# A gated cross-attention block with routed experts: GpSimd's low-weight rows behind VectorE's second norm, routing groups and scatters earlier, tables over four steps

## What is computed

```
x = x + tanh(g_xattn) * xattn(ctx, layernorm(x))
    # s = layernorm(ctx)*g1+b1; t = layernorm(.)*g2+b2; q = t Wq; k = s Wk; v = s Wv
    # softmax(q k^T / sqrt(8)) v, 16 heads, then Wfc
xf = layernorm(x)
gates = sigmoid(xf @ Wg); vals, idx = top_k(gates, 2); vals = vals / vals.sum()
shared = (silu(xf @ Ws1) * (xf @ Ws3)) @ Ws2
routed = sum over the two chosen experts: weight * (silu(xf @ We1) * (xf @ We3)) @ We2
x = x + tanh(g_ffn) * (shared + routed) / 3
```

## Time and profile before

| | us |
|---|---|
| median of 3 runs | 461.3 |
| lowest, highest | 459.54, 461.4 |
| the profiled execution | 458.93 |
| its span | 457.1 |

### The profile page before, as it was taken

How to read it: one execution, slowest core, us unless ns; L and a number is a source line. 1 busy time by engine, 2 the same in 40 slices (tenths; PEclk the granted TensorE clock), 3 DMA queues, 4 the chain that set the end, 5 groups by cost and what they waited for, 6 DMA issues and landing times.

```text
span 457.1 us, 10667 instructions
## 1 busy us (share of the span) xinstructions
PE 359.4 (79%) x3718; PEld 269.3 (59%) x3718; DVE 344.0 (75%) x866; ACT 264.9 (58%) x601; POOL 279.4 (61%) x375
## 2 busy tenths in 40 slices
PE   0689999997998969899869710999999999999400
PEld 0356666665765647676658600777777777778300
DVE  2559999999999998998848820576777777777447
ACT  1257777776687746687656600355555555556244
POOL 3373666666379966888647773017777777777700
PEclk9999999999799988899979865799999999999855
DMA  4920699991001110000001155113236666541179
GB/s 110 275 77 3 261 375 377 391 385 41 13 27 49 36 48 25 27 25 26 25 23 42 49 217 165 52 52 94 93 95 231 232 231 230 210 184 52 47 264 298
DMA packets 39331, 62.36 MB, mean 136 GB/s; under 512 B 5936, under 2 KB 23344, under 8 KB 39280
## 3 DMA queue, kind: packets, MB, share of 16 engines
q1 hardware_dynamic: 32704, 51.12, 32.6%
q0 software_dynamic: 4992, 10.30, 6.7%
q10 hardware_dynamic: 1584, 0.27, 0.4%
HBM read 18.32 MB, written 31.56 MB: 109 GB/s over the span
## 4 chain that ended last, share of the span: by engine, by line
PE 41%; DVE 25%; issue 13%; POOL 13%; ACT 4%; DMA 3%; POOLq 0%; DVEq 0%; SPq 0%; ACTq 0%
POOL expert_rows L545 7%; PE ps L1215 6%; PE ps L1216 5%; PE ps L1217 5%; DVE row_max L935 5%; PE ps L1252 3%; DVE inv_sum L976 3%; PE ps L1158 3%; POOL token_sums L622 3%; PE ps L1112 3%; DVE norm L900 2%; PE ps L1240 2%; PE ps L1238 2%; PE ps L1239 2%; DVE x_sb L1061 2%
## 5 line engine op out<-in xcount | busy, mean ns | idle before, releaser
L622 POOL DMA_INDIRECT token_sums<-prob,y_at x92 | 94.5, 1027 | 60.7 <-DVE prob L1035 38.8
L545 POOL DMA_INDIRECT expert_rows<-c_sb,pos x64 | 64.3, 1005 | 16.9 <-issue 16.8
L587 POOL TENSOR_TENSOR k_mask<-k_st,head_mask 128x512 f32<-128x512 f32 x32 | 33.5, 1046 | 43.8 <-ACT k_st L695 43.6
L739 ACT ACTIVATE h_hi<-prob 128x512 fp32r<-128x512 f32 x62 | 38.3, 634 | 36.5 <-DVE prob L998 36.5
L732 ACT ACTIVATE probT<-ps 128x512 f32<-128x512 f32 x62 | 36.9, 598 | 30.6 <-PE ps L1217 27.0
L1112 PE MATMUL ps<-k_mask,qT 32*64 32x256 f32 x512 | 46.0, 431 | 9.4 <-DVE prob L941 7.7
L998 DVE TENSOR_TENSOR prob<-ps,probT 128x512 f32<-128x512 f32 x62 | 40.2, 684 | 13.9 <-ACT probT L732 10.9
L935 DVE TENSOR_REDUCE row_max<-ps 128x16 f32<-128x1024 f32 x32 | 38.9, 1216 | 11.0 <-PE ps L1112 10.9
L1003 DVE TENSOR_TENSOR h_lo<-prob,h_hi 128x512 fp32r<-128x512 f32 x62 | 40.5, 689 | 3.4 <-ACT h_hi L739 0.4
L1019 DVE TENSOR_TENSOR xT_lo<-ps,xT_hi 128x512 fp32r<-128x512 f32 x23 | 15.9, 692 | 35.9 <-ACT xT_hi L744 35.9
L703 ACT ACTIVATE probT<-ps 128x512 f32<-128x512 f32 x64 | 35.2, 595 | 10.5 <-PE ps L1158 10.4
(11 more groups left out here) (164 smaller groups left out, 977.1 us busy)
## 6 DMA issues: line engine op xcount, KB each, us to landing
expert_rows<-zeros SPq DMA_DIRECT2D x36, 520.0 KB, 5.2
c_sb<-expert_rows SPq DMA_DIRECT2D x23, 260.0 KB, 2.7
wbuf_hi<-w_hi SPq DMA_DIRECT2D x15, 384.0 KB, 2.9
wbuf_lo<-w_lo SPq DMA_DIRECT2D x15, 384.0 KB, 3.4
w_raw<-in_L_ffn_We_dram SPq DMA_DIRECT2D x24, 128.0 KB, 4.2
c_sb<-token_sums SPq DMA_DIRECT2D x8, 256.0 KB, 4.7
xT_lo<-token_sums SPq DMA_DIRECT2D x8, 256.0 KB, 4.9
out_dram<-x_sb SPq DMA_DIRECT2D x8, 256.0 KB, 4.9
```

The lines of the kernel that those rows point to most:

```text
L545: pool.indirect_dma_start(out=xs, out_offset=bass.IndirectOffsetOnAxis(pos[:, k, i:i + 1], 0), in_=c_sb[:, i, :], in_offset=None).then_inc ...
L622: pool.indirect_dma_start(out=ys, out_offset=bass.IndirectOffsetOnAxis(y_at[:, s, k:k + 1], 0), in_=yrows[:, s % 2, k * D:(k + 1) * D], in ...
```

## The change

Four things. GpSimd's step has a new wait, for xn2_ready of tile t-4, ahead of w_lo and the scale piece, in steps 4 to 14, where no tile is scattered. The routing tables are moved up: GATE_STEP by one step, COUNT_STEP and RANK_STEP by two, and all five parts of `routing` run in COUNT_STEP itself. Scatters start at step 15 instead of 18, one tile a step, and so the table for the steps behind NT = 32 is another one; tiles 24 to 27 no longer wait for unit 4. The tables are written in steps 0 to 3 in four parts. TensorE waits for gate_exp behind the logits matmul instead of ahead of it, and has a new wait for pos_ready at step 35.

```
-        GATE_STEP = [14, 22, 30, 34, None]
-        COUNT_STEP = [16, 24, 32, 36, None]
-        RANK_STEP = [17, 25, 33, 37, None]
+        GATE_STEP = [13, 21, 29, 33, None]
+        COUNT_STEP = [14, 22, 30, 34, None]
+        RANK_STEP = [15, 23, 31, 35, None]
...
-            if 18 <= t < NT:
-                return range(t - 18, t - 17)
-            return {NT: [14], NT + 1: [15], NT + 2: [16, 17], NT + 3: [18, 19], NT + 4: [20, 21],
-                    NT + 5: [22, 23]}.get(t, [])
+            if 15 <= t < NT:
+                return range(t - 15, t - 14)
+            return {NT: [17, 18], NT + 1: [19, 20], NT + 2: [21, 22], NT + 3: [23, 24], NT + 4: [25, 26],
+                    NT + 5: [27]}.get(t, [])
...
-            def tables():
+            def tables(part):
...
+                if part == 0:
...
                     pool.iota(c_sb[:, :, D].rearrange("p (c k) -> p c k", k=CH), [[CT, NC], [1, CH]], base=0,
                               channel_multiplier=CH, allow_small_or_imprecise_dtypes=True).then_inc(table_step, 1)
+                if part == 1:
                     pool.wait_ge(table_step, 1)
...
+                if part == 2:
                     pool.wait_ge(table_step, 2)
...
+                if part == 3:
                     pool.iota(steps512[:, :, :], [[T, E], [ROWS, JMAX - 1]], base=ROWS, **exact)
...
+                i = t - 4
+                if within(i) and not scatter_tiles(t):
+                    pool.wait_ge(xn2_ready, i + 1)
                 if splits(t):
                     pool.wait_ge(w_hi_ready, t - WS_FROM + 1)
...
-                if t == 0:
-                    tables()
+                if 0 <= t < 4:
+                    tables(t)
...
             def unit(n):
-                if n == TAIL_UNIT:
-                    for i in range(24, 28):
-                        scatter(i)
                 if n == TAIL_UNIT + 1:
...
                 for g, last in enumerate(COUNT_STEP):
-                    if last is not None and last - 1 <= t <= last:
-                        for part in (range(0, 3) if t < last else range(3, 5)):
+                    if t == last:
+                        for part in range(5):
                             routing(g, part)
...
                     pe.wait_ge(xT_f32_ready, i + 1)
+                    pe.matmul(p_logit[:, i, :], xT_f32[:, b, :], wg_raw[:, :], start=True,
+                              stop=True).then_inc(logits_ready, 1)
                     if t > NT and t in GATE_STEP:
                         pe.wait_ge(gate_exp, GATE_STEP.index(t) + 1)
-                    pe.matmul(p_logit[:, i, :], xT_f32[:, b, :], wg_raw[:, :], start=True,
-                              stop=True).then_inc(logits_ready, 1)
...
+                    if t > NT + 1 and t in RANK_STEP:
+                        pe.wait_ge(pos_ready, RANK_STEP.index(t) + 1)
                     pe.transpose(x2_bank(t), c_sb[:, i, 0:D], ident[:, :]).then_inc(xn2_turned, 1)
```

52 lines of the change are left out of this document (26 added, 26 removed).

## The result

The changed kernel takes 467.8 us (median of 4 runs, 466.95 to 469.02) and the kernel before, on the same chip, 460.4: **ratio 1.0164, 95% interval 1.0121 to 1.0207**. I had forecast 462.4 with a range of 456.5 to 467.0. The profiled execution took 466.99 us, its span is 464.9 us against 457.1: +7.8 for a sum of +1.1.

What follows compares the result with a forecast made beforehand. VectorE and GpSimd excluding each other in attention, then the scatter chain with GpSimd's 7.3 us backlog, were taken as bounds. Terms summed to +1.1 on the 461.3 us median: 462.4 us, no change, range 456.5 to 467.

Steps and rivals of the forecast that it cites:

- (a): Step 1: tables written over four steps cut TensorE's idle time; -0.8 us, bounds 0 and -0.9.
- (b): Steps 4 to 14: w_lo behind the second norm no longer holds VectorE; -2.5 us, bounds 0 and -4.3.
- that rival: Attention: the gate has no effect, xT_lo moves onto the second norm, steps stay at 5.74; 464.9 us, chance 0.06.
- the rival of the pow rows: Steps 5 to 14: VectorE's small rows wait for a pow of 1.03 us; +3.1 us, 464.4 us, chance 0.04.
- (c): Group 0's routing in one piece ahead of row_max 14; +2.0 us, bounds +0.8 and +3.
- (d): Scatters from step 15, three steps earlier, lengthen those steps; +1.9 us, bounds +0.5 and +3.
- (e): Group 1's routing in one piece, steps 22 and 23; +2.0 us, bounds 0 and +3.
- (f): Group 2's routing in one piece ahead of row_max 30, steps 30 to 32; +3.0 us, ends +1.7 and +5.5.
- my own point of decision: TensorE's waits of steps 30 and 33: its clock falls from about 2.5 us of idle time.
- rival "slower": Steps 30 and 33: TensorE's waits lower its clock, half-speed chain to the last places row; 466.4 us, chance 0.27.
- (g): Group 3 behind attention: TensorE waits at steps 33 and 35, last places row later; +2.8 us, bounds +0.8 and +4.8.
- (h): End of the scatters: GpSimd's backlog is gone when the last places row comes; -7.3 us.

Runs made afterwards that it cites:

- changed_filled_full: The changed kernel with 30, 48 and 30 idle TensorE identity turns ahead of the scores of steps 15, 23 and 31; 463.2 us, ratio to before 1.0029.
- a_b_only: The kernel before with only the split tables and w_lo behind the second norm, routing and scatters where they stood; 455.5 us, ratio to before 0.9877.
- groups01_merged: The changed kernel with routing groups 2 and 3 put back as in the kernel before; 459.1 us, ratio to before 0.9951.
- best_filled: a_b_only with scatters from step 17, those behind attention one tile earlier, idle turns in step 34 and ahead of steps 16 and 24; 452.4 us, ratio 0.9795.
- changed_tail_filled: The changed kernel with 14 and 30 idle identity turns in group 3's waits of steps 33 and 35; 466.0 us, ratio to before 1.0061.
- a_b_scatter_from_17: a_b_only with scatters starting in step 17 instead of 18; 453.9 us, ratio to before 0.9816.

## Why the prediction was wrong

**(a) and (b): right in kind, 1.3 us too cautious.** Steps 7 to 11 took 5.54 us, the x norm 0.34. Over steps 2 to 12 (b) gained 2.2 us, where I had 2.5.

Step 1 took 5.89 us for 7.85, so (a) was 2.0 here, beyond its bound of 0.9; in the other kernels with the split tables step 1 took 5.84 to 6.90, which makes it 1.0 to 2.0. The difference is in TensorE's own rows. Its 32 matmuls on v_st took 1.08 us there in the kernel before (L1202, from 30.26), 0.63 in the changed one, and again 1.08 in changed_filled_full, whose step 1 took the 6.90. So 1.0 us of (a) is there in every one of these executions, near its 0.87, and up to 1.0 more goes with how long TensorE's rows stay long. Why they do is not shown. The last 0.4 of the 4.6 was there before row_max 1. In time a_b_only is 5.7 us faster by its ratio (4.0 to 7.3), more than my 3.3.

The gate works, which ends that rival. GpSimd's pow of 1.02 us beside the small rows at the step's end (57.81, above) did not lengthen the step, which ends the rival of the pow rows. I had read the rule of the Trainium skill too widely (SBUF — State Buffer, section on the two separate sides): it names as VectorE's instructions that take the shared pair those in a 2-port performance mode or with two SBUF inputs, and lists no aggregate rows among them. The trace agrees with that rule for w_lo and for k_mask (VectorE's row with two SBUF inputs, 1.83 us for 0.22), and not for the pow beside c_sb, which kept its 0.34 us.

**(c), (d) and (e): right in kind, +7.8 for +5.9.** (d) measured 2.4 for 1.9, which is within the scatter of single profiles, the two mergings 5.4 for 4.0. Of these 1.4 the meetings with k_mask can be 1.1, the 3.4 us that the two pieces lose to them less the 2.3 lost before. "Exposed: 1.74 + 1.2" was worked out for group 0. For group 1 I carried it over, though its wait is 6.45 us here, and had already been 4.27 us before (ahead of the scores at 168.04), which I had not looked at.

**(f): the step of the forecast that failed.** "I take 0.8" and "+3.0, with +1.7 and +5.5 as ends, the latter if the clock falls" put the likeliest case on the wrong side of my own point of decision. TensorE waited 4.14 us, not "2.7 us or more": the first half alone had made 1.79, and the second half's 1.74 on top make 3.5, so my own rows already lay beyond the 2.51 us that had let the clock fall. Of the kernel before, the one group that had kept its clock lost it: +5.6 us at the table load, 5.1 in the time of two kernels.

Half of the 5.6 lies ahead of row_max 31 and half behind it. Ahead, from row_max 29 to 31, it is 2.8 (16.01 us for 13.17), for the 2.5 of my 1.74 and 0.8, with 1.5 us lost to k_mask where I took 0.8. Behind, from row_max 31 to the table load, it is 2.8 (10.17 us for 7.40), for the 0.7 of the count. TensorE's granted clock is 0.50 from 220 to 224 us, and in the kernel before it is 1.00 up to the table load. So the term that I had at nothing is 2.1 us behind the wait, where TensorE's rows run at half clock; no run prices the clock alone there. My own terms, 1.74, 0.8 and 0.7, also make 3.2 and not 3.0.

The rival "slower" had 5.2 for it, and a time of 466.4. That this is near 467.8 is in part luck: its other terms are off by -1.3 (a, b), +1.9 (c to e), -1.3 (g) and +2.9 (behind the scatters).

**(g): right in its sum, +3.3 for +2.8, not in its parts.** Both waits came (2.42 and 4.12 us, said 2.4 and 4.5) and both lowered the clock. But group 3's place costs 5.9 us, of which 2.7 are the clock, and 2.9 come back from group 2's piece, where I had 3.6 and 0.8.

**(h): right.** 9.3 us from places to last scatter, with a gap, -7.2 for -7.3. What I left out is that the same scatters would then meet the weight copies, which hang on the last places row: +1.1 in the landing. Neither of the two edits that moved the copies turned that into time.

**Behind the scatters: put at nothing, +2.9.** This is the largest single miss of the sum, and part of it may be the luck of two executions. The landing is 1.1 of it. Then 0.6 us lies between the turned rows and the last scatter of sums (150.8 us for 150.2: TensorE was back at full clock 8.2 us behind its first turn, for 7.1), and 1.1 us behind that, where the last load of sums took 5.08 us for 3.08 in the chain. Over the 18 profiles, whose kernels differ there in nothing but the place of the copies in two, the first of these stretches took 149.6 to 152.2 us and the second 22.9 to 24.3. From last scatter to the end it was 177.6 to 181.2 us; the kernel before (178.2) has nearly the shortest and the changed one (181.1) nearly the longest. So beyond the landing nothing there is shown to be the change's.

The sum is off by 6.7: -1.3, +1.9, +2.6, +0.5, +0.1 and +2.9. "Slower by the clock" was the right case; it had a chance of 0.27 and should have been the first, since the pieces were known to be longer than the one that had let the clock fall. And "It decides from about 2.5 us of idle time" had a counterexample in the kernel before: a wait of 1.73 us ahead of 258.88, 1.0 us of matmuls and a wait of 0.88, and from 261 to 263 us the granted clock was 0.50.

## What to carry to other kernels

An idle stretch of TensorE is priced by itself and by the slow rows behind it; when an edit lengthens one that had kept its clock, count both, and look at each such wait of the kernel before. A piece of another engine's work costs least where TensorE already waits or has a backlog of its own, so two halves beside its chain beat one whole ahead of it. And when a backlog is removed, ask what else is released by the same event, and whether the backlog can be had by starting its work a step earlier, which here gave the gain without moving what feeds it.

## What the runs showed of the hardware

The clock does not follow from the length of the last wait alone. It stayed at 1.00 behind waits of 1.79 and 1.81 us (groups01_merged), each with matmuls of 512 columns behind it. It fell behind one of 1.73 us in the kernel before (258.88, with a wait of 0.88 us shortly behind), one of 1.87 (best_filled, with a wait of 0.43 shortly behind) and one of 1.55 (changed_filled_full) that had 30 turns of the identity ahead of it.

13 turns of a 128x128 identity took 1.64 us, 0.13 each, less than half of the 0.29 that the kernel's own transposes average (298 ns in L1162, whose mean mixes rows at both clocks). 14 and 30 such turns in waits of 2.42 and 4.12 us, and nothing else changed, held the granted clock at 1.00 from 230 to 258 us (changed_tail_filled), where the changed kernel has 0.85 at 234 to 238 us and 0.56 at 250 to 254.

A VectorE row of routing that meets GpSimd's k_mask took 0.97 to 2.04 us for 0.22 (the changed kernel's three pieces). Whether it is met is decided by when the piece comes, and can differ between executions of nearly the same rows: 1.83 us in a_b_only, 0.23 in a_b_scatter_from_17.

The spread from run to run differs between these kernels: a_b_scatter_from_17 ran from 449.7 to 454.6 us, groups01_merged, over 12 runs for 6, from 457.8 to 459.6. Why is not shown.
